# A new table of PE's side jobs, DMA transposes in thirds, and k doubled by ACT instead of by the rope addition

## What is computed

```python
def _L1_attn_ref(x, wq, wk, wv, wo):
    xq = (x @ wq).reshape(Bx, Tx, N_HEAD, HEAD_DIM)        # N_HEAD = 32, HEAD_DIM = 64
    xk = (x @ wk).reshape(Bx, Tx, N_KV_HEAD, HEAD_DIM)     # N_KV_HEAD = 8
    xv = (x @ wv).reshape(Bx, Tx, N_KV_HEAD, HEAD_DIM)
    xq = xq * cos + _rotate_half(xq) * sin
    xk = xk * cos + _rotate_half(xk) * sin
    xk = jnp.repeat(xk, 4, axis=2)
    xv = jnp.repeat(xv, 4, axis=2)
    scores = jnp.einsum('bqhd,bkhd->bhqk', xq, xk) * scale
    scores = jnp.where(causal[None, None], scores, -jnp.inf)
    probs = jax.nn.softmax(scores, axis=-1)
    out = jnp.einsum('bhqk,bkhd->bqhd', probs, xv).reshape(Bx, Tx, N_HEAD * HEAD_DIM)
    return out @ wo

x = x + _L0_attn_ref(_layernorm(x), ...)      # first layer, not touched
x = x + _L0_ffn_ref(_layernorm(x), ...)
x = x + _L1_attn_ref(_layernorm(x), wq, wk, wv, wo)
x = x + _L1_ffn_ref(_layernorm(x), w_fc, w_proj)
```

## Time and profile before

| what | value |
|---|---|
| median of 3 runs | 609.13 us (608.51 to 610.8) |
| the profiled execution, its own time | 610.31 us |
| its span | 608.5 us |
| instructions in the span | 16334 |
| granted TensorE clock, mean | 0.992 |
| SP's queue (q1) | 311680 packets, 86.66 MB |
| steps of the attention loop | 64, between 142 and 560 us |

### The profile page before, as it was taken

The page is one execution under the profiler, slowest core; times in us unless marked ns, Lnnn a source line. Parts: engine busy times, 40 slices in busy tenths (PEclk is TensorE's granted clock), DMA queues, the critical chain, the costliest instruction groups (busy, mean ns, idle before and its releaser), DMA issues.

```text
span 608.5 us, 16334 instructions
## 1 busy us (share of the span) xinstructions
PE 557.9 (92%) x6880; PEld 481.3 (79%) x6880; DVE 458.2 (75%) x751; ACT 436.8 (72%) x608; POOL 452.5 (74%) x371
## 2 busy tenths in 40 slices
PE   5999999987879999999989999999999997996898
PEld 4878898976767898888878888888888976885666
DVE  4686766777767888887877877788788875675897
ACT  0524401249688889889788988988988888974876
POOL 3034426447998998999899899899999977874423
PEclk9999999999999999999999999999999999997989
DMA  8160004006999999999999999999999999998001
GB/s 283 62 209 0 2 21 83 11 2 138 183 175 194 193 183 195 194 199 196 180 181 198 219 196 195 181 212 184 196 177 210 197 184 203 190 177 158 1 27 44
DMA packets 317193, 91.76 MB, mean 151 GB/s; under 512 B 305984, under 2 KB 316224, under 8 KB 317120
## 3 DMA queue, kind: packets, MB, share of 16 engines
q1 hardware_dynamic: 311680, 86.66, 82.1%
q10 hardware_dynamic: 5440, 4.06, 2.6%
HBM read 13.11 MB, written 1.05 MB: 23 GB/s over the span
## 4 chain that ended last, share of the span: by engine, by line
PE 41%; POOL 18%; DVE 16%; DMA 11%; ACT 6%; SPq 4%; issue 4%; POOLq 0%; ACTq 0%; DVEq 0%
POOL p_lo L501 13%; PE PS L1278 12%; DMA pT_lo<-p_lo 10%; PE PS L1537 7%; DVE small L1097 6%; PE PS L1557 4%; PE PS L1411 3%; SPq L402 3%; ACT probs L715 2%; POOL roped L490 2%; PE PS L1388 2%; PE PS L1393 2%; PE PS L1389 2%; PE PS L1301 2%; PE PS L1561 2%
## 5 line engine op out<-in xcount | busy, mean ns | idle before, releaser
L501 POOL TENSOR_TENSOR p_lo<-probs,p_hi 128x2048 f16<-128x2048 f32 (+7 forms) x128 | 303.6, 2390 | 34.4 <-DMA pT_lo<-p_lo 18.8
L715 ACT ACTIVATE probs<-PS,small 128x128 f32<-128x128 f32 (+7 forms) x256 | 173.5, 743 | 43.7 <-DVE small L1097 41.6
L1097 DVE TENSOR_REDUCE small<-PS 128x2 f32<-128x2048 f32 (+7 forms) x128 | 172.8, 1351 | 21.4 <-PE PS L1537 20.9
L724 ACT CAST p_hi<-probs 128x2048 f16<-128x2048 f32 (+7 forms) x128 | 145.8, 1160 | 5.0 <-DMA pT_hi<-p_hi 4.9
L1557 PE MATMUL PS<-v_hi,pT_hi 128*128 128x65 f16 x1152 | 78.8, 194 | 1.3 <-DMA pT_hi<-p_hi 1.3
L1561 PE MATMUL PS<-v_lo,pT_hi 128*128 128x64 f16 x1152 | 78.7, 195 | 0.0
L1537 PE MATMUL PS<-k_hi,q_hi 64*128 64x512 f32 (+3 forms) x384 | 74.0, 381 | 2.5 <-ACT probs L715 2.5
L1557 PEld LDWEIGHTS PS<-v_hi,pT_hi 128*128 128x128 f16 x1152 | 73.9, 99 | 3.0 <-issue 1.4
L1561 PEld LDWEIGHTS PS<-v_lo,pT_hi 128*128 128x128 f16 x1152 | 72.5, 98 | 0.5
L1537 PE MATMUL PS<-k_lo,q_hi 64*128 64x512 f32 (+3 forms) x384 | 66.0, 339 | 0.0
L1537 PE MATMUL PS<-k_hi,q_lo 64*128 64x512 f32 (+3 forms) x384 | 66.0, 339 | 0.0
(11 more groups left out here) (210 smaller groups left out, 1349.6 us busy)
## 6 DMA issues: line engine op xcount, KB each, us to landing
wgu_nat<-L_ffn_w_gate_up SPq DMA_DIRECT2D x2, 1024.0 KB, 9.4
wo_nat<-L_attn_wo ACTq DMA_DIRECT2D x7, 256.0 KB, 3.1
wkq_nat<-L_attn_wq ACTq DMA_DIRECT2D x6, 256.0 KB, 5.1
x<-L_attn_x SPq DMA_DIRECT2D x4, 256.0 KB, 3.9
wdn_nat<-L_ffn_w_down SPq DMA_DIRECT2D x1, 1024.0 KB, 11.0
wfc_nat<-L_ffn_w_fc SPq DMA_DIRECT2D x1, 1024.0 KB, 6.7
wpj_nat<-L_ffn_w_proj SPq DMA_DIRECT2D x1, 1024.0 KB, 9.8
pT_hi<-p_hi SPq DMA_TRANSPOSE x64, 5.5
```

What stands on the lines that cost most here:

```text
L501: nc.gpsimd.tensor_tensor(p16_lo[G % 2][:, cols], probs[G % 2][:, cols], p16_hi[G % 2][:, cols], ALU.subtract).then_inc(p_lo_done, 1)
L715: nc.scalar.activation(probs[G % 2][:, start:start + w], PS[:, src:src + w], ACT.Exp, bias=nmax[:, 4 * (G % 2) + u:4 * (G % 2) + u + 1]).t ...
L724: nc.scalar.copy(p16_hi[G % 2][:, cols], probs[G % 2][:, cols]).then_inc(p_hi_done, 1)
L1097: nc.vector.tensor_reduce(nmax[:, first:first + 2], both_heads(G, part), AX.X, ALU.max, negate=True).then_inc(nmax_done, 1)
```

## The change

Four things are changed.

1. **Thirds.** p16_hi and p16_lo of a step become one tile of 36 blocks, the low half behind the high half, and so does the turned tile pT. SP issues three transposes of 12 blocks for each step in place of two of 18. The first has 12 high blocks, the second the last 6 high and the first 6 low ones, the third 12 low ones. The first waits for part 0 of the high half alone where that has 12 blocks or more (`r` of 1 to 3), otherwise for both parts. The second waits for all of the high half and for part 0 of the low one, the third for part 1 of the low one. ACT, POOL and PE wait for the thirds that they touch.
2. **k by ACT.** POOL's two rope additions of a tile become one, of 320 columns, with k written once. ACT copies k beside itself for four tiles at a time (`k_again`, 128 x 4 x 64), and PE's transposes of k wait for that (`k_twice`).
3. **The table.** `RAMP_JOBS` and `JOBS` are new; `LAST_JOBS` is not. The output projection goes in the order 1, 2, 0, 3 in all groups, and jobs 1 and 2 wait for three of the four transposed outputs instead of for four. The split of its weights moves from n = 2 to n = 1 on ACT and POOL.
4. **Addresses.** Some tiles move to make room, with nothing else changed about them.

```diff
-    p16_hi = [sb(f"p16_hi{b}", 186 + 9 * b, [18 * P], F16) for b in range(2)]
-    p16_lo = [sb(f"p16_lo{b}", 190.5 + 9 * b, [18 * P], F16) for b in range(2)]
-    pT_hi = [sb(f"pT_hi{b}", kb, [18, P], F16) for b, kb in enumerate((26, 30.5, 104.5))]
-    pT_lo = [sb(f"pT_lo{b}", kb, [18, P], F16) for b, kb in enumerate((60, 128, 132.5))]
+    p16 = [sb(f"p16_{b}", 186 + 9 * b, [36 * P], F16) for b in range(2)]
+    p16_hi = [t[:, 0:18 * P] for t in p16]
+    p16_lo = [t[:, 18 * P:36 * P] for t in p16]
+    pT = [sb(f"pT_{b}", kb, [36, P], F16) for b, kb in enumerate((26, 128, 104.5))]
...
-        JOBS = {0: ("q1t0", "q1t1", "r0"), 1: ("r1", "r2", "ot2"), 2: ("r3", "r4", ""), 3: ("ot3", "r5", "r6"),
-                4: ("kt0", "wo0", "r7"), 5: ("", "wo1", "kt1"), 6: ("q0t0", "wo2", "q0t1"), 7: ("ot0", "wo3", "ot1")}
+        JOBS = {0: ("q1t0", "r0", "q1t1"), 1: ("r1", "r2", "ot2"), 2: ("r3", "wo1", ""), 3: ("", "r4", "ot3"),
+                4: ("kt0", "wo2", "r5"), 5: ("ot0", "r6", "r7"), 6: ("q0t0", "wo0", "kt1"), 7: ("q0t1", "wo3", "ot1")}
...
-            def transpose_hi(G):
-                sp.wait_ge(p_hi_done, 2 * G + 2)
-                sp.dma_start(pT_hi[G % 3][:], p16_hi[G % 2][:], transpose=True).then_inc(pT_hi_landed[G % 3], 16)
-
-            def transpose_lo(G):
-                sp.wait_ge(p_lo_done, 2 * G + 2)
-                sp.dma_start(pT_lo[G % 3][:], p16_lo[G % 2][:], transpose=True).then_inc(pT_lo_landed[G % 3], 16)
+            def turn_third(G, k):
+                sp.dma_start(pT[G % 3][:, THIRD * k:THIRD * (k + 1), :], p16[G % 2][:, THIRD * k * P:THIRD * (k + 1) * P],
+                             transpose=True).then_inc(pT_landed[k][G % 3], 16)
...
                 if G >= 3:
                     sp.wait_ge(pv_done, G - 2)
-                transpose_hi(G)
-                transpose_lo(G)
+                sp.wait_ge(p_hi_done, 2 * G + (1 if 2 * blocks(G, 0) >= THIRD else 2))
+                turn_third(G, 0)
+                sp.wait_ge(p_hi_done, 2 * G + 2)
+                sp.wait_ge(p_lo_done, 2 * G + 1)
+                turn_third(G, 1)
+                sp.wait_ge(p_lo_done, 2 * G + 2)
+                turn_third(G, 2)
...
-                both = [P, 2, HEAD]
-                nc.gpsimd.tensor_tensor(roped[:, t, 0:P].rearrange("p (h d) -> p h d", h=2),
-                                        t_cos[b][:, 0:1, :].broadcast_to(both),
-                                        t_sin[b][:, 0:1, :].broadcast_to(both), ALU.add)
-                nc.gpsimd.tensor_tensor(roped[:, t, P:3 * P], t_cos[b][:, 1:5, :].rearrange("p h d -> p (h d)"),
-                                        t_sin[b][:, 1:5, :].rearrange("p h d -> p (h d)"),
+                nc.gpsimd.tensor_tensor(roped[:, t, HEAD:3 * P], t_cos[b][:].rearrange("p h d -> p (h d)"),
+                                        t_sin[b][:].rearrange("p h d -> p (h d)"),
                                         ALU.add).then_inc(rope_added, 1)
...
+            def k_again(gg, half):
+
+                act.wait_ge(rope_added, NT * gg + 4 * (half + 1))
+                tiles = slice(4 * half, 4 * half + 4)
+                nc.scalar.copy(roped[:, tiles, 0:HEAD], roped[:, tiles, HEAD:P]).then_inc(k_twice, 1)
...
             nc.scalar.activation(col(60), s_sum[:, 0:1], ACT.Exp)
+            k_again(0, 1)
             qk_high("k", 0, 1, 4, 2)
...
+                if n == 3 and g < NG - 1:
+                    k_again(g + 1, 0)
+                if n == 6 and 0 < g < NG - 1:
+                    k_again(g + 1, 1)
```

More of the change, by code:

```diff
@@ L733, in _ @@
             v_high(2)
+            k_again(0, 0)
             qk_high("k", 0, 0, 7, 0)
@@ L756, in _ @@
                 p_high(G, 0)
+                if n == 5 and g == 0:
+                    k_again(1, 1)
                 if n == 5 and g + 2 < NG:
@@ L1544, in pv @@
             def pv(G, b):
-                g, buf, turn = G // 8, G % 3, G // 3 + 1
+                g, buf = G // 8, G % 3
                 o = bank(b)
                 first = True
-                for pT, landed in ((pT_hi, pT_hi_landed), (pT_lo, pT_lo_landed)):
-                    pe.wait_ge(landed[buf], 16 * turn)
+                for low in range(2):
                     for part in range(2):
```

52 lines of the change are left out of this document (33 added, 19 removed).

## The result

The changed kernel takes 628.19 us, median of four runs (627.28 to 629.8), against 608.82 us (608.09 to 610.8) for the kernel before in the same job: ratio 1.0316, 95% interval 1.0282 to 1.0349. The forecast was 609.0 with 596 to 624 as its range, so it was wrong. The profiled execution took 629.8 us.

What follows compares the result with a forecast made beforehand. The prediction took SP's stream of transposes, plus returning stalls, to bound the loop. It summed 610.3 + 1.1 - 4.4 - 1.5 + 4.7 = 610.2 us for the profiled execution, 1.2 above the median, so 609.0, range 596 to 624.

Steps and rivals of the forecast that it cites:

- the stream of transposes: SP's queue in the loop: 36 blocks a step, said to bound it together with returning stalls, 6.45 us a step.
- SP's queue covers a wait of some tenths: wo1 in step 2, needing its split a step earlier: costed at nothing, up to 1 us a group if uncovered.
- The rival: New table makes PE wait, wo1 behind POOL's split or kt1 behind ACT's copy: 1 us a group, 615; chance 0.10.
- -4.4 - 1.5 + 4.7 = -1.2 us: SP's queue: earlier feeding in steps 0 to 11 (-4.4) and in the steady gaps (-1.5), added DMA starts (+4.7).
- the start of a DMA: SP's queue: one more start a step, 0.09 us each, +4.7 us over 52 steps.
- the first rival: Another engine bounds and thirds relieve SP's issues, with faster issue per block or smaller stalls: 14 us less, 595; chance 0.28.
- The rival of a fixed part of up to 0.42 us: SP's queue, every step: each DMA start costs up to 0.42 us, 631.2 or 630 in median terms; chance 0.20.
- its small case: SP's queue: a start costs 0.04 us and all gaps go, 52 x 0.05 + 2.5 us less, 604.
- 0.87 forecast: POOL's single rope addition of 320 columns takes 0.87 us, saving 0.32 a tile; costed at nothing on the bound part.
- +1.1 forecast: Ahead of the loop: ACT's second copy behind the Exp table delays k_hi by 1.0, plus 0.1 for the first copy.
- "Hidden.": ACT in the loop: fourteen of 16 copies of k, 0.40 us each, cost nothing, as ACT is busy 45.30 of 52 us.

Runs made afterwards that it cites:

- less_dma: The kernel before with 14 of the 18 blocks of the low part transposed from step 3 on; 605.33 us, ratio 0.9915.
- wo_early: The changed kernel with the split of wo, on ACT and POOL, in step 0 of a group in place of step 1; 613.33 us, ratio 1.0024.
- old_start_mid: oldtable with POOL doubling k for the first group and three pairs awaited by projections 1 and 2 of the last group but one; 607.4 us, ratio 0.9926.
- best_halves: old_start_mid with two transposes of 18 blocks a step in place of three of 12; 610.28 us, ratio 0.9997.
- thirds_only: The changed kernel with the old table, POOL's two rope additions and no copy of k; 609.25 us, ratio 0.997.
- kcopy_only: The kernel before with one rope addition a tile and k copied by ACT; 612.27 us, ratio 1.0011.
- oldtable: The changed kernel with the table of before, ACT's second copy of k in step 5; thirds and copy stay; 611.12 us, ratio 0.9999.
- halves: The changed kernel with two transposes of 18 blocks a step in place of three of 12; 627.17 us, ratio 1.0287.
- wo_start: wo_early with k doubled by POOL for the first eight tiles, in place of ACT's copies; 610.27 us, ratio 1.0.
- table_only: The changed kernel with transposes of 18 blocks, POOL's two rope additions and no copy of k; 631.62 us, ratio 1.0345.
- copy_late: wo_start with ACT's first copy of k for the second group behind the probabilities of step 3; 608.74 us, ratio 0.9949.

## Why the prediction was wrong, point by point

**What bounds the loop.** "So the loop is bound by the stream of transposes" was half right. It explains the excursions of a group over 51.24 us, and less_dma removed them; by the queue's pace alone a step was 6.45 us. But the next floor lies close under it at 6.40, and the prediction put it at 6.2 from PE's busy time. Busy time left out the cycle PE, DVE, ACT, PE, in which no engine needs to be full. An even queue with gaps of 0.04 us showed that SP was full, not that it had slack to lend to a wait on another engine.

**The table: the step that failed.** "and SP's queue covers a wait of some tenths. Nothing for it, and up to 1 us a group if the cover fails." The rival had the right place, wo1 behind POOL's split, and 0.10 as its chance. Measured are 2.64 us a group, six times, 15.9 us, and wo_early took 2.9% back with that one edit. Two things were wrong in it. The length of the wait was taken from the slack of POOL and PE, 1.8 us of 52, and a mean slack says nothing of when an instruction comes in an engine's order: a pair of rope additions, 3.11 us of subtraction and 1.27 us of split stood between PE and its weights. And the cover was thought to be one engine's queue; with another bound 0.9% under it, a stand of PE moved the scores, the row maxima and the exponentials by its full length (2.67 us in step 2 for a stand of 2.64).

**Thirds.** Forecast -4.4 - 1.5 + 4.7 = -1.2 us. Measured -0.3% alone, about -2 us, -0.7%, about -4, between old_start_mid and best_halves, and nothing clear of the noise in the other pairs. The term of the wrong sign is the start of a DMA, +0.09 us each: from step 12 to the last SP's issues took 324.8 us in all in the kernel before and 314.4 in thirds_only, for the same 1,872 blocks and with 52 more starts. The other pairs have the same sign: 325.5 and 314.3 (kcopy_only, oldtable), 324.4 and 314.0 (best_halves, old_start_mid), 310.9 and 305.3 (halves, the changed kernel). The shortest third took 1.27 us, the shortest 18 blocks 2.41; 12/18 of that is 1.6. This is the first rival's clue, a third issues faster per block. The rival of a fixed part of up to 0.42 us is refuted: it needed thirds of over 1.9 us, and the median is 1.77 in the changed kernel, stalls included:

```profile
L408 SPq DMA_TRANSPOSE pT<-p x192: 1276/1769/4790, 145.1 to 574.4; - x192
```

By the Trainium skill, "DMA: Bandwidth & Descriptors", Rules for kernel authors, many small transfers should be joined into one; it names 64 KB as the size under which one pays mostly overhead. The parts here are 393 KB and the wholes 590 KB (12 and 18 blocks of 32.8 KB), so the rule gave no price for this cut. In the trace the parts issued faster than the whole, and could start earlier. The fixed cost of 2.0 us that the prediction set beside the rule is given in its section for DMAs that GpSimd issues; these are issued by SP.

One number of the first rival was added wrongly: its small case counted all 2.5 us of gaps, of which 1.5 were in the forecast already, so by its own terms it comes to 605, not 604.

**Rope addition.** 0.87 forecast, 0.878 measured, and nothing gained, as forecast, while SP and the cycle bound.

**k by ACT, ahead of the loop.** +1.1 forecast, 3.1 us in the profiled execution (first scores 135.45 against 132.54, first row maxima 137.04 against 133.93). The forecast term was right and another was missing. 0.5 of the 3.1 was there by the table load (129.61 against 129.10), 1.2 are the copy's, as in wo_early and halves, and 1.4 came with the lower clock, which the prediction put at nothing: it didn't reckon PE's idle time of 2.68 us. In the time the start shows as about 0.2% between wo_early and wo_start.

**k by ACT, in the loop.** "Hidden." Once it isn't: in step 3 of the first group the rope addition it waits for is made in the same step, and exponentials are queued behind it. The first group takes 1.1 us more in the changed kernel, and the copy alone gives that: 52.77 in kcopy_only and 52.67 in oldtable, but 51.31 in table_only, against 51.61 before. copy_late gained 0.5% by moving it. The prediction weighed the copy's 0.40 us and not what it waits for.

**The sum.** The medians differ by 19.4 us, and the pieces give it: 6 x 2.74 = 16.4 in the groups 1 to 6, of which 15.9 are the stands at wo1; 3.1 ahead of the loop; 1.1 in the first group; -2.1 in the last; 0.9 in the tail. Three pieces are left open, and no run isolates them: the 0.4 us by which a group of wo_early (52.1) is still longer than one of before (51.69), mostly in the steps 2 and 6 (6.32 and 6.98 against 5.99 and 6.60); the last group, shorter by 2.1; and the tail.

## What to carry to other kernels

When a table moves a job to an earlier slot, walk the queue of the engine that prepares its input: add up what stands ahead of it there, in the order of the program, against the time when the consumer comes. Mean slack doesn't answer that. A copy moved to another engine is costed by what it waits for and what is queued behind it, not by its own length. And before one queue is called the bound, look for the cycle through the buffers (here scores, row maxima, exponentials): here two bounds within 1% of each other left no cover, and they showed only when each was cut alone and both together.
